# Typed gather pass of a graph network: weighting moved to the head of a turn, block indices and tables made one block ahead

## The chip, the cores and the metric

The kernel runs on one core of one Trainium2 chip. The metric is the device time of one execution in microseconds (us); lower is better. All names of engines are those of the profile: PE is the matrix engine, PEld its weight loads, DVE the vector engine, ACT the scalar engine, POOL the engine that issues the gathers, SP the one that issues plain transfers.

## The reference, cut to what matters

Four graph layers run one after the other on 12,500 nodes and 412,500 edges sorted by target node. The change lies in the first one, in its sum over edges:

```
W = einsum('rb,bio->rio', comp, basis)         # one 64x64 matrix for each of 64 edge types
msg = x[src] * edge_weight
s = segment_sum(msg, edge_type * N + dst)      # by type and target node
h = relu(einsum('rni,rio->no', s, W) + bias)
x = layernorm(x + batchnorm(h + relu(x @ res_w.T + res_b)))
```

The kernel first makes the table Yd of x times W for every node and type, so that the sum becomes, for each edge, the row Yd[src, type] times the edge's weight, added to the edge's target node. This sum over edges is the typed pass. The three later layers (two convolutions, then a pass over wide rows) use the same edges.

## The kernel before, in words

The program is a row of phases. `ytab` (to 560 us) builds Yd; `typed_pass` (lines 363 to 554, from 560 to 5688 us) makes the sum; then come `dense0` and the other layers, which the change doesn't touch.

The typed pass goes over 129 blocks of 25 times 128 edges (the last one has 23 times 128). Tiles are double buffered by j, the parity of the block. In every block there are two products of PE:

- **The groups.** For each of the 25 columns k of a block, PE multiplies two one-hot matrices (lines 527 and 529, a pair of matmuls) to build, in bf16, a matrix that later layers read back from DRAM. The one-hot matrices are written by DVE in 4 groups (`group`, lines 462 to 466: 6, 6, 6 and 7 columns) into a ring of two. PE waits for the group (semaphore gb). Every third column PE tells by a semaphore cm0, cm1 or cm2 that three columns are done ("a triple"; triples 0 to 8), ACT copies the triple out of PSUM (line 549), and PE may use that part of PSUM again two triples later (semaphore av). So column 24, the last of a block, waits for ACT's copy of triple 6. DVE may overwrite a part of the ring when the first triple of the following group is done: group 1 waits for triple 0, group 2 for triple 2, group 3 for triple 4, and group 0 of the next block for triple 6.
- **The sum by nodes.** POOL gathers 25 times 128 rows of Yd by the indices ix into gv (line 428), DVE multiplies them by the edge weights pw (line 501), DVE also writes the one-hot oh of the target nodes (line 491), and PE adds up gv times oh over the block (line 535, 50 records of f32 matmuls for 25 columns). The result is added to acc by DVE (`add`, line 471).

Each engine walks through the blocks in its own fixed order; `turn(b, j, i)` is one block on one engine, and `short_blocks` runs turn 0, a loop, and the last two turns.

DVE in turn b, before: group 0; `prep` for block b+1 (line 445 makes the indices ix, lines 447 to 455 the tables cl, vw, rl); group 1; the one-hot oh (line 491); group 2; `add` of block b-1; `weight` of block b+1 (line 474, into PSUM); group 3; the weighting of gv (line 501).

PE in turn b, before: the 25 pairs of the groups, then, when the weighting is done (semaphore mul), the sum by nodes, which ends with an increment of the semaphore pe.

POOL in turn b waits for pe of block b-2 (gv is free) and for ix of block b, and then issues 25 gathers.

SP in turn b, which isn't changed: it waits for pw of block b, issues the load of the table of block b+2 into mt[j] (line 398, 63.0 KB; source node, type, target, first target and weight of every edge), then waits for ACT's last copy of block b and issues the store of the block's matrix to Aj (line 405, 3062.5 KB). In the order of SP's stream the load for block b+2 thus stands right behind the store of block b-1:

```
def turn(b, j, i):
    if type(b) is not int or b + 2 < NA:
        b = reg(e, b)
        e.wait_ge(sm["pw"], reg(e, b + 1))
        load(b + 2, j)
    store(b, j, i)
```

Of the kernel before, what the change touches and what calls it, by code (L numbers as in the profile page):

```python
# [8 lines left out]
ALU = mybir.AluOpType  # L9
# [5 lines left out]
P = 128  # L15
# [15 lines left out]
KA = 25  # L31
NA = -(-E // (P * KA))
LA = -(-E // P) - (NA - 1) * KA
# [16 lines left out]
def build(nc, x, xT, meta, metaA, dstp, d0, d0s, jrow, half, dstr, wgt, efT, base, basa, ident, iota, basis, compT, l0v, res_wT,  # L50
          W1, l1b1, W2, l1b2, mW1, mb1, mW2, mb2, uW1, ub1, uW2, ub2, out):
    ctx = ExitStack()
    with ctx:
# [49 lines left out]
        def bc_f(v, t=NT, f=64):  # L103
            return v.unsqueeze(2).to_broadcast([P, t, f])

        def bc_t(v, t, f):
            return v.unsqueeze(1).to_broadcast([P, t, f])
# [40 lines left out]
        def at(b, n):  # L148
            return type(b) is int and b == n

        def reg(e, v):
            return v if type(v) is int else e.snap(v)
# [210 lines left out]
        def typed_pass(sm, block, s):  # L363
# [4 lines left out]
            gv = [big[:, KA * 65 * j:KA * 65 * (j + 1)].rearrange("p (k f) -> p k f", f=65) for j in range(2)]  # L368
            o0, o1 = KA * 130, KA * 130 + KA * P
            oh = big[:, o0:o1].rearrange("p (k n) -> p k n", n=P)  # L370
# [6 lines left out]
            rl = [loc(f"rl{j}", [P, KA]) for j in range(2)]  # L377
# [8 lines left out]
            ag = [PS[0][0:65, P * j:P * (j + 1)] for j in range(2)]  # L386
            pw = [PS[0][:, 2 * P + KA * j:2 * P + KA * (j + 1)] for j in range(2)]
            iof = PS[1][:, 0:W * NT]
# [44 lines left out]
            def vector(e):  # L433
                for h in range(4):
                    n = min(P, W * NT - P * h)
                    nc.vector.tensor_scalar(iof[:, P * h:P * h + n], io[:, 0:n], float(P * h), None,
                                            ALU.add).then_inc(sm["io"], 1)
                nc.vector.memset(oex[1][:, GM - 1, :], 0.0).then_inc(sm["io"], 1)
                nc.vector.memset(olo[1][:, GM - 1, :], 0.0).then_inc(sm["io"], 1)
                for j in range(2):  # L440
                    nc.vector.memset(gv[j][:, :, 64:65], 1.0).then_inc(sm["io"], 1)

                def prep(b, j, loaded, n):
                    e.wait_ge(sm[f"m{j}"], loaded)
                    nc.vector.scalar_tensor_tensor(out=ix[j][:, :], in0=mt[j][:, 0:KA], scalar=float(NR),
                                                   in1=mt[j][:, KA:2 * KA], op0=ALU.mult, op1=ALU.add).then_inc(sm["ix"], 1)
                    nc.vector.tensor_scalar(cl[j][:, 0:KA], mt[j][:, 0:KA], 7, None, ALU.logical_shift_right)
                    nc.vector.tensor_scalar(cl[j][:, KA:2 * KA], mt[j][:, 0:KA], P - 1, None, ALU.bitwise_and)
                    nc.vector.tensor_tensor(vw[j][:, 0:KA], mt[j][:, 2 * KA:3 * KA], mt[j][:, 3 * KA:4 * KA], ALU.subtract)
                    nc.vector.tensor_tensor(vw[j][:, KA:2 * KA], mt[j][:, 3 * KA + 1:4 * KA + 1], mt[j][:, 2 * KA:3 * KA],  # L450
                                            ALU.subtract)
                    nc.vector.tensor_tensor(rl[j][:, :], mt[j][:, 2 * KA:3 * KA], mt[j][:, 3 * KA:3 * KA + 1].to_broadcast([P, KA]),
                                            ALU.subtract).then_inc(sm["pr"], 1)
                    e.wait_ge(sm["pr"], n)
                    nc.vector.scalar_tensor_tensor(out=two(vw[j][:, :]), in0=two(vw[j][:, :]), scalar=float(NT),
                                                   in1=bc_t(cl[j][:, 0:KA], 2, KA), op0=ALU.mult,
                                                   op1=ALU.add).then_inc(sm["vw"], 1)

                def group(j, g, n):
                    r, k = g % 2, chunks[g]  # L460
                    m = k.stop - k.start
                    nc.vector.tensor_tensor(one[r][:, 0:m, :], bc_t(iof, m, W * NT), bc_f(vw[j][:, k], m, W * NT), ALU.is_equal)  # L462
                    nc.vector.tensor_tensor(oex[r][:, 0:m, :], bc_t(iof[:, 0:NT], m, NT),
                                            bc_f(vw[j][:, KA:2 * KA][:, k], m, NT), ALU.is_equal)
                    nc.vector.tensor_tensor(olo[r][:, 0:m, :], bc_t(iof[:, 0:P], m, P),  # L465
                                            bc_f(cl[j][:, KA:2 * KA][:, k], m, P), ALU.is_equal).then_inc(sm[f"gb{g}"], 1)

                def add(b, j):
                    at = e.value_load(basea[0:1, bass.ds(b, 1)], min_val=0, max_val=N)
                    dst = acc[0:65, bass.ds(at, P)]  # L470
                    nc.vector.tensor_tensor(dst, dst, ag[j], ALU.add).then_inc(sm["acc"], 1)

                def weight(j):
                    nc.vector.tensor_copy(pw[j], wgt_[j]).then_inc(sm["pw"], 1)

                def turn(b, j, i):
                    first, last, b = at(b, 0), at(b, NA - 1), reg(e, b)
                    n, c0, c1, c2 = reg(e, b + 1), reg(e, 3 * b), reg(e, 3 * b + 1), reg(e, 3 * b + 2)
                    kn = LA if last else KA
                    if not first:  # L480
                        e.wait_ge(sm["cm0"], c0)
                    e.wait_ge(sm["vw"], n)
                    group(j, 0, n)
                    if not first:
                        e.wait_ge(sm["mul"], b)
                    if not last:
                        prep(b + 1, 1 - j, 16 * (i + 1 + j), reg(e, b + 2))
                    e.wait_ge(sm["cm0"], c1)
                    group(j, 1, n)
                    e.wait_ge(sm["pe"], n)  # L490
                    nc.vector.tensor_tensor(oh[:, 0:kn, :], bc_t(iof[:, 0:P], kn, P), bc_f(rl[j][:, 0:kn], kn, P), ALU.is_equal)
                    e.wait_ge(sm["cm2"], c1)
                    group(j, 2, n)
                    if not first:
                        add(b - 1, 1 - j)
                    if not last:
                        weight(1 - j)
                    e.wait_ge(sm["cm1"], c2)
                    group(j, 3, n)
                    e.wait_ge(sm[f"g{j}"], 16 * KA * i + 16 * kn)  # L500
                    nc.vector.tensor_tensor(gv[j][:, 0:kn, 0:64], gv[j][:, 0:kn, 0:64], bc_f(pw[j][:, 0:kn], kn, 64),
                                            ALU.mult).then_inc(sm["mul"], 1)

                e.wait_ge(sm["io"], 8)
                prep(0, 0, 16, 1)
                weight(0)
                short_blocks(e, turn, NA)
                e.wait_ge(sm["pe"], NA + 1)
                add(NA - 1, 0)

            def tensor(e):
                e.sem_inc(sm["pe"], 1)

                def turn(b, j, i):
                    first, last, b = at(b, 0), at(b, NA - 1), reg(e, b)
                    n, done = reg(e, b + 1), [reg(e, 3 * b + h) for h in range(4)]
                    for k in range(LA if last else KA):
                        g, t = min(k // GC, GN - 1), k // 3
                        c = k - GC * g
                        r = g % 2  # L520
                        q = 2 + 3 * ((j + t) % 2) + k % 3
                        if c == 0:
                            e.wait_ge(sm[f"gb{g}"], n)
                        if k % 3 == 0:
                            if t >= 2 or not first:
                                e.wait_ge(sm[f"av{(t - 2) % 3}"], done[(t - 2) // 3 + 1])
                        nc.tensor.matmul(PS[q][:, 0:W * NT], olo[r][:, c, :], one[r][:, c, :], start=True, stop=False)  # L527
                        pr, pc = (r, c - 1) if c else (1 - r, GC - 1 if g else GM - 1)
                        mm = nc.tensor.matmul(PS[q][:, 0:NT], olo[pr][:, pc, :], oex[pr][:, pc, :], start=False, stop=True)  # L529
                        if k % 3 == 2 or k == (LA if last else KA) - 1:  # L530
                            mm.then_inc(sm[f"cm{t % 3}"], 1)
                    e.wait_ge(sm["mul"], n)
                    kn = LA if last else KA
                    for k in range(kn):
                        mm = nc.tensor.matmul(ag[j], gv[j][:, k, :], oh[:, k, :], start=(k == 0), stop=(k == kn - 1))  # L535
                    mm.then_inc(sm["pe"], 1)
                short_blocks(e, turn, NA)

            def scalar(e):
# [1161 lines left out]
```

## Time and profile before

| what | us |
| --- | --- |
| median of 3 runs | 13430.48 |
| lowest and highest run | 13422.02, 13433.54 |
| profiled execution, span from the first to the last instruction | 13426.1 |
| typed pass in it | about 560 to 5688 |
| busy in the span: PE, DVE, POOL, ACT | 7285.8, 6792.6, 6380.1, 2832.8 |

No separate time of the profiled execution beyond its span is shown; the span lies 4.4 us below the median of the runs. The page gives, for each engine, how long it was busy; in a timeline a row reads: start in us, duration in us, engine, line, operation, what it writes and reads, shapes, how many instructions were merged into the row, and in brackets how long the engine had been idle before and what released it. "Remote" as a releaser means a semaphore update that the profile can't tie to an instruction's end; "issue" means that it shows nothing that was waited for. Starts of matmuls are measured, their ends are modelled.

### The profile page before, as it was taken

Reading aid. Unit: us, or ns where it says so; the run is one execution under the profiler, and the core shown is the slowest. Engines: PE = TensorE matmul, PEld = TensorE weight load, DVE = VectorE, ACT = ScalarE, POOL = GpSimd, SP = SyncE. Lnnn points to the kernel's source line nnn. Section 1 sums busy time; section 2 is a strip of 40 time slices with the busy share of each in tenths; the row PEclk is TensorE's granted clock in tenths of the full one; section 3 lists DMA queues with packets and bytes.
Section 4 is the critical chain, followed back from the end, with each engine's and each line's share of the span. In section 5 each row is a group of like instructions: output and inputs, shape, how many; then the busy total and the mean of one; then the engine's idle time right before and its main releaser. Section 6 shows DMA issues by size and latency. Waiting matters only on the chain. (4 is left out here: it accounts for less than half of the span.)

```text
span 13426.1 us, 144231 instructions
## 1 busy us (share of the span) xinstructions
PE 7285.8 (54%) x52956; PEld 5571.9 (42%) x52956; DVE 6792.6 (51%) x8156; ACT 2832.8 (21%) x2654; POOL 6380.1 (48%) x6717
## 2 busy tenths in 40 slices
PE   9755545555555455589999994333333333333334
PEld 4333333333333333379989994222222222222223
DVE  5566666666666666632232224444444444444445
ACT  4333333333333333320000001111111111111112
POOL 4456565656565656400000004555555665555564
PEclk9877777677767666689999997666666666666667
DMA  9732323232323233379979994333333333333332
GB/s 388 290 107 97 106 97 106 98 106 98 106 97 106 97 105 99 106 267 370 370 292 370 371 370 116 87 88 88 88 86 85 87 88 88 87 88 87 85 86 66
DMA packets 480426, 2020.11 MB, mean 150 GB/s; under 512 B 193465, under 2 KB 246136, under 8 KB 354776
## 3 DMA queue, kind: packets, MB, share of 16 engines
q1 hardware_dynamic: 205304, 1283.59, 27.3%
q0 software_dynamic: 206272, 317.25, 10.1%
q10 hardware_dynamic: 68768, 418.23, 8.6%
q8 instruction: 46, 0.75, 0.0%
q14 instruction: 36, 0.29, 0.0%
HBM read 1385.92 MB, written 632.61 MB: 150 GB/s over the span
## 5 line engine op out<-in xcount | busy, mean ns | idle before, releaser
L1289 POOL DMA_INDIRECT big<-Pd,mt x3223 | 3041.0, 944 | 2127.8 <-DMA mt<-in_meta 1186.2
L428 POOL DMA_INDIRECT big<-Yd,ix x3223 | 3041.5, 944 | 2069.5 <-PE ps L535 1095.7
L462 DVE TENSOR_TENSOR ring<-ps,vw 128x2940 bf16<-128x2940 f32 (+1 forms) x516 | 1725.9, 3345 | 1761.8 <-PE ps L529 1516.3
L527 PE MATMUL ps<-ring 128*128 128x490 bf16 x3223 | 1427.4, 538 | 1999.5 <-DVE ring L465 1190.3
L1316 DVE TENSOR_TENSOR ps<-ps,big 128x1024 f32<-128x1024 f32 x403 | 494.9, 1229 | 2656.3 <-remote 2397.2
L527 PEld LDWEIGHTS ps<-ring 128*128 128x128 bf16 x3223 | 416.3, 129 | 2802.4 <-issue 1835.0
L1423 PE MATMUL ps<-idt,total 128*128 128x128 f32 x135 | 63.8, 473 | 2716.1 <-DVE total L1329 2716.1
L535 PE MATMUL ps<-big 128*65 128x128 f32 x6446 | 1149.9, 346 | 555.3 <-issue 554.6
L535 PEld LDWEIGHTS ps<-big 128*65 128x65 f32 x6446 | 1045.9, 185 | 651.7 <-issue 644.9
L1423 PEld LDWEIGHTS ps<-idt,total 128*128 128x128 f32 x135 | 24.4, 181 | 2814.7 <-DVE total L1329 2814.7
L549 ACT ACTIVATE Z<-ps 128x1470 bf16<-128x1470 f32 (+1 forms) x584 | 800.1, 1399 | 1790.2 <-PE ps L529 755.2
L549 ACT ACTIVATE big<-ps 128x1470 bf16<-128x1470 f32 (+1 forms) x576 | 786.5, 1397 | 1748.2 <-remote 833.6
L666 PE MATMUL ps<-big,cb 128*128 128x192 bf16 x12642 | 1065.5, 246 | 0.0
L666 PEld LDWEIGHTS ps<-big,cb 128*128 128x128 bf16 x12642 | 1036.4, 98 | 11.5
L1380 ACT ACTIVATE big<-ps 128x1024 bf16<-128x1024 f32 x269 | 275.2, 1023 | 2976.7 <-issue 2270.5
L529 PE MATMUL ps<-ring 128*128 128x98 bf16 x3223 | 850.5, 264 | 0.0
L1416 PE MATMUL ps<-big 128*128 128x384 bf16 x2151 | 565.9, 425 | 297.1 <-DVE big L1325 297.1
L1408 PE MATMUL ps<-qw,te 128*128 128x128 f32 x3216 | 510.3, 306 | 256.6 <-issue 256.4
L1115 POOL MEMSET acc<- 64x128 f32 x1 | 0.2, 198 | 1274.1 <-POOLq L115 1274.1
L1408 PEld LDWEIGHTS ps<-qw,te 128*128 128x128 f32 x3216 | 480.0, 222 | 260.1 <-issue 251.1
L1212 POOL TENSOR_TENSOR X<-X,vb 128x6272 f32<-128x6272 f32 x1 | 13.5, 13489 | 1174.2 <-POOLq L115 1174.2
L666 PE MATMUL ps<-big 128*128 128x192 bf16 x6370 | 550.0, 247 | 28.4 <-DMA big<-Aj 28.4
(215 smaller groups left out, 11561.0 us busy)
## 6 DMA issues: line engine op xcount, KB each, us to landing
Yd<-big SPq DMA_DIRECT2D x196, 1024.0 KB, 8.8
Aj<-Z SPq DMA_DIRECT2D x65, 3062.5 KB
big<-Aj SPq DMA_DIRECT2D x130, 1531.2 KB, 8.3
cb<-Aj ACTq DMA_DIRECT2D x130, 1531.2 KB, 8.5
Aj<-big SPq DMA_DIRECT2D x64, 3062.5 KB
cb<-Aj SPq DMA_DIRECT2D x128, 1531.2 KB, 8.4
Z<-Aj ACTq DMA_DIRECT2D x128, 1531.2 KB, 8.5
dr<-in_dstr SPq DMA_DIRECT2D x135, 1152.0 KB
```

Source lines behind the costliest of these rows:

```text
L428: e.indirect_dma_start(gv[j][:, k, 0:64], None, table, bass.IndirectOffsetOnAxis(ap=ix[j][:, k:k + 1], axis=0)).then_inc(sm[f"g{j}"], 16)
L462: nc.vector.tensor_tensor(one[r][:, 0:m, :], bc_t(iof, m, W * NT), bc_f(vw[j][:, k], m, W * NT), ALU.is_equal)
L527: nc.tensor.matmul(PS[q][:, 0:W * NT], olo[r][:, c, :], one[r][:, c, :], start=True, stop=False)
L529: mm = nc.tensor.matmul(PS[q][:, 0:NT], olo[pr][:, pc, :], oex[pr][:, pc, :], start=False, stop=True)
L535: mm = nc.tensor.matmul(ag[j], gv[j][:, k, :], oh[:, k, :], start=(k == 0), stop=(k == kn - 1))
L549: nc.scalar.activation(aw[j][:, :, 3 * t:3 * t + m, :], trip[(j + t) % 2][:, :, 0:m, :], ACT.Copy).then_inc(sm[f"av{t % 3}"], 1)
L666: last = nc.tensor.matmul(pa[j], buf[2 * j + h][:, D * c:D * c + P], wz[:, t, :], start=(t == 0), stop=(t == NT - 1))
L1289: e.indirect_dma_start(gv[j][:, k, :], None, Pd, bass.IndirectOffsetOnAxis(ap=mt[j][:, k:k + 1], axis=0)).then_inc(sm[f"g{j}"], 16)
L1316: nc.vector.tensor_tensor(step[q], step[q], G[j][:, SW * q:SW * (q + 1)], ALU.add).then_inc(sm[f"x{q}"], 1)
L1380: nc.scalar.activation(part[q][:, 0], step3[q], ACT.Relu).then_inc(sm[f"hi{q}"], 1)
L1408: last = nc.tensor.matmul(step[q][:, c * P:(c + 1) * P], te[j][:, k * P:(k + 1) * P], qw[j][k // HK][:, :], start=True, stop=True)
L1416: last = nc.tensor.matmul(ag, oh[j][:, k, :], parts[q][:, 3 * P * c:3 * P * (c + 1)], start=(k == 0), stop=(k == chunks - 1))
```

## The change

The reference and all phases but `typed_pass` stay as they are. Three engines' orders are touched:

- DVE, turn b, after: the weighting of gv of block b; `indices` of block b+2 (behind a wait for the load of that block's table); groups 0, 1, 2, 3 without anything between them; `prep` of the tables of block b+2; the one-hot oh of block b+1 (`targets`, behind a wait for PE's sum of block b); `add` of block b; `weight` of block b+2. Ahead of turn 0 the indices, tables and weights of blocks 0 and 1 and the one-hot of block 0 are made.
- PE, turn b, after: the sum by nodes of block b first, then the 25 pairs of block b.
- POOL, SP and ACT are as before.

```
-                def prep(b, j, loaded, n):
+                def indices(j, loaded):
                     e.wait_ge(sm[f"m{j}"], loaded)
                     nc.vector.scalar_tensor_tensor(out=ix[j][:, :], in0=mt[j][:, 0:KA], scalar=float(NR),
                                                    in1=mt[j][:, KA:2 * KA], op0=ALU.mult, op1=ALU.add).then_inc(sm["ix"], 1)
+
+                def prep(j, n):
                     nc.vector.tensor_scalar(cl[j][:, 0:KA], mt[j][:, 0:KA], 7, None, ALU.logical_shift_right)
...
+                def targets(j, n, kn):
+                    e.wait_ge(sm["pe"], n)
+                    nc.vector.tensor_tensor(oh[:, 0:kn, :], bc_t(iof[:, 0:P], kn, P), bc_f(rl[j][:, 0:kn], kn, P), ALU.is_equal)
+
                 def turn(b, j, i):
-                    first, last, b = at(b, 0), at(b, NA - 1), reg(e, b)
+                    first, last, more = at(b, 0), at(b, NA - 1), type(b) is not int or b + 2 < NA
+                    nxt = LA if at(b, NA - 2) else KA
+                    b = reg(e, b)
                     n, c0, c1, c2 = reg(e, b + 1), reg(e, 3 * b), reg(e, 3 * b + 1), reg(e, 3 * b + 2)
                     kn = LA if last else KA
+                    e.wait_ge(sm[f"g{j}"], 16 * KA * i + 16 * kn)
+                    nc.vector.tensor_tensor(gv[j][:, 0:kn, 0:64], gv[j][:, 0:kn, 0:64], bc_f(pw[j][:, 0:kn], kn, 64),
+                                            ALU.mult).then_inc(sm["mul"], 1)
+                    if more:
+                        indices(j, 16 * i + 32)
                     if not first:
                         e.wait_ge(sm["cm0"], c0)
                     e.wait_ge(sm["vw"], n)
                     group(j, 0, n)
-                    if not first:
-                        e.wait_ge(sm["mul"], b)
-                    if not last:
-                        prep(b + 1, 1 - j, 16 * (i + 1 + j), reg(e, b + 2))
                     e.wait_ge(sm["cm0"], c1)
                     group(j, 1, n)
-                    e.wait_ge(sm["pe"], n)
-                    nc.vector.tensor_tensor(oh[:, 0:kn, :], bc_t(iof[:, 0:P], kn, P), bc_f(rl[j][:, 0:kn], kn, P), ALU.is_equal)
                     e.wait_ge(sm["cm2"], c1)
                     group(j, 2, n)
-                    if not first:
-                        add(b - 1, 1 - j)
-                    if not last:
-                        weight(1 - j)
                     e.wait_ge(sm["cm1"], c2)
                     group(j, 3, n)
-                    e.wait_ge(sm[f"g{j}"], 16 * KA * i + 16 * kn)
-                    nc.vector.tensor_tensor(gv[j][:, 0:kn, 0:64], gv[j][:, 0:kn, 0:64], bc_f(pw[j][:, 0:kn], kn, 64),
-                                            ALU.mult).then_inc(sm["mul"], 1)
+                    if more:
+                        e.wait_ge(sm["gb3"], n)
+                        prep(j, reg(e, b + 3))
+                    if not last:
+                        targets(1 - j, reg(e, b + 2), nxt)
+                        add(b, j)
+                    if more:
+                        weight(j)
 
                 e.wait_ge(sm["io"], 8)
-                prep(0, 0, 16, 1)
-                weight(0)
+                for j in range(2):
+                    indices(j, 16)
+                    prep(j, j + 1)
+                    weight(j)
+                targets(0, 1, KA)
                 short_blocks(e, turn, NA)
...
                     n, done = reg(e, b + 1), [reg(e, 3 * b + h) for h in range(4)]
+                    e.wait_ge(sm["mul"], n)
+                    kn = LA if last else KA
+                    for k in range(kn):
+                        mm = nc.tensor.matmul(ag[j], gv[j][:, k, :], oh[:, k, :], start=(k == 0), stop=(k == kn - 1))
+                    mm.then_inc(sm["pe"], 1)
                     for k in range(LA if last else KA):
...
-                    e.wait_ge(sm["mul"], n)
-                    kn = LA if last else KA
-                    for k in range(kn):
-                        mm = nc.tensor.matmul(ag[j], gv[j][:, k, :], oh[:, k, :], start=(k == 0), stop=(k == kn - 1))
-                    mm.then_inc(sm["pe"], 1)
```

## Rows read from the trace of the kernel before

**Rows 1.** The page of the whole run: its span.

```profile
span 13426.1 us, 144231 instructions
```

**Rows 2.** Groups by line, 2000 to 5000 us: busy, mean ns | idle before, releasers.

```profile
L428 POOL DMA_INDIRECT big<-Yd,ix x1896 | 1789.0, 944 | 1211.7 <-PE ps L535 657.0 <-issue 554.7
...
L535 PE MATMUL ps<-big 128*65 128x128 f32 x3800 | 683.0, 348 | 326.9 <-issue 326.4
```

**Rows 3.** Timeline of one turn, all engines, 3009 to 3047 us.

```profile
3009.04 0.35 SPq L405 DMA_DIRECT2D Aj<-Z  x1
3009.93 0.34 SPq L398 DMA_DIRECT2D mt<-in_metaA  x1
...
3012.36 0.94 POOL L428 DMA_INDIRECT big<-Yd,ix  x1 [9.25 <-PE ps L535]
...
3012.76 3.22 DVE L462 TENSOR_TENSOR ring<-ps,vw 128x2940 bf16<-128x2940 f32 x1 [11.55 <-PE ps L529]
...
3017.44 3.48 DVE L491 TENSOR_TENSOR big<-ps,rl 128x3200 f32<-128x3200 f32 x1
...
3019.34 2.96 ACT L549 ACTIVATE big<-ps 128x1470 bf16<-128x1470 f32 x2 [3.74 <-issue]
...
3020.84 3.21 DVE L462 TENSOR_TENSOR ring<-ps,vw 128x2940 bf16<-128x2940 f32 x1
...
3025.51 0.28 DVE L471 TENSOR_TENSOR acc<-acc,ps 65x128 f32 x1
...
3027.34 3.73 DVE L462 TENSOR_TENSOR ring<-ps,vw 128x3430 bf16<-128x3430 f32 x1 [1.46 <-PE ps L529]
...
3032.76 1.81 DVE L501 TENSOR_TENSOR big<-big,ps 128x1600 f32<-128x1600 f32 x1
...
3034.26 0.29 PE L529 MATMUL ps<-ring 128*128 128x98 bf16 x1
...
3037.15 1.48 ACT L549 ACTIVATE big<-ps 128x1470 bf16<-128x1470 f32 x1 [6.86 <-remote]
3037.15 3.22 DVE L462 TENSOR_TENSOR ring<-ps,vw 128x2940 bf16<-128x2940 f32 x1 [2.58 <-remote]
...
3038.95 4.69 PE L535 MATMUL ps<-big 128*65 128x128 f32 x26
...
3042.32 0.95 POOL L428 DMA_INDIRECT big<-Yd,ix  x1 [0.30 <-issue]
...
3042.49 0.21 DVE L455 SCALAR_TENSOR_TENSOR vw<-vw,cl 128x50 f32<-128x50 f32 x1
...
3046.94 4.05 PE L535 MATMUL ps<-big 128*65 128x128 f32 x22 [0.38 <-issue]
3046.96 2.10 ACT L549 ACTIVATE big<-ps 128x1470 bf16<-128x1470 f32 x2 [8.33 <-remote]
```

**Rows 4.** Transfers, 3010 to 3016 us: packets, bytes, packets by size.

```profile
DMA packets 98, 2.40 MB, mean 400 GB/s; under 512 B 0, under 2 KB 0, under 8 KB 0
```

**Rows 5.** Transfers, 3017 to 3019 us: packets by size, then SP's queue.

```profile
DMA packets 289, 0.20 MB, mean 99 GB/s; under 512 B 224, under 2 KB 224, under 8 KB 289
...
q1 hardware_dynamic: 160, 0.06, 11.6%
```

**Rows 6.** Timeline of the first turns, 563 to 602 us.

```profile
563.17 3.19 SPq L398 DMA_DIRECT2D mt<-in_metaA  x3
...
565.03 0.19 DVE L445 SCALAR_TENSOR_TENSOR ix<-mt 128x25 int32<-128x25 int32 x1 [0.62 <-DMA mt<-in_metaA]
...
602.00 1.48 ACT L549 ACTIVATE Z<-ps 128x1470 bf16<-128x1470 f32 x1 [13.22 <-remote]
```

**Rows 7.** Timeline of the pass's end, 5675 to 5690 us.

```profile
5675.55 6.50 PE L535 MATMUL ps<-big 128*65 128x128 f32 x46
5677.68 0.34 SPq L405 DMA_DIRECT2D Aj<-Z  x1
...
5689.24 0.51 SPq L892 DMA_DIRECT2D wA<-in_res_wT  x1
```

## The prediction, made before the changed kernel had run

> **What bounds the kernel now.** The span is 13426.1 us [rows 1]; I make the sum against it, and add the 4.4 us by which the median of the runs (13430.5) lies above it. A measurement of this kernel can tell about 0.2% (27 us) from no change. Only the typed pass is touched.
>
> First the groups by line [rows 2]. In 3000 us POOL waited for PE's sum by nodes (line 535) in 76 turns (1896 gathers at 25 a turn), so a turn takes 3000 / 76 = 39.5 us, and these waits come to 657.0 / 76 = 8.6 us a turn. A chain that holds both POOL and PE thus sets the turn. The timeline of a turn shows it [rows 3]:
>
> - Gathers start at 3012.36, released by the end of the sum, and the last is issued at 3042.32: 30.9 us of gathering.
> - PE's record for the last matmul of triple 6 starts at 3034.26 and should be done near 3034.5, yet ACT and DVE, both waiting for it, start at 3037.15. ACT's copy of triple 7 starts only at 3046.96, though all matmuls but column 24 stood ready behind it. In the same time the sum by nodes issues 26 matmuls from 3038.95, falters, and runs the last 22 in one piece from 3046.94. So PE's completions are held back while gathers go on, from about 22 us after their start, and come free at 3046.96, 34.6 us after it. I have no name for the mechanism, but it follows the gathers: in the first turns, where gathering began near 566 and didn't pause, ACT's copy came 13.22 us late at 602.00 [rows 6]; in the last turn, without any gathers, the sum runs through, 46 matmuls in 6.50 us [rows 7].
>
> The turn before is then 34.6 (gathers and hold) + 4.05 (the 22 last matmuls) + 0.85 (to the next gather) = 39.5 us, as observed. DVE has slack: its idle 11.55 us ahead of 3012.76.
>
> **The change part by part.** PE's stream is the same ring of sum, groups, sum, groups; only its cut into turns moves. POOL's two gates are met in the same place: indices exist long before, and the sum releases it. The instructions of DVE are the same in number, so nothing is saved or added in busy time. What moves:
>
> 1. *The one-hot oh (3.4 us) leaves the gap between groups 1 and 2.* Call x the start of group 1 (3012.76). Group 1 ends at x+4.8 (3017.53). Group 2 then waits for triple 2 (ACT starts on it at 3019.34): x+6.6, instead of 3020.84. Group 2 takes 4.7 (3020.84 to 3025.51, where `add` begins), then 1.8 for triple 4 (to 3027.34), then group 3 takes 5.5: it ends at x+18.6 instead of x+20.1. Gain 1.5 us. `add` and `weight` (0.28 and about as much less, 0.5 together at most) were covered by the 1.8 and are now open.
> 2. *The tail of DVE's turn.* Tables 0.8 (group 0, indices and tables run from 3037.15 to 3042.70, less 4.7 for the group), oh 3.4, add and weight 0.5, weighting 1.81 [rows 3]: the weighting ends at x+25.1, and the sum may start then. Before, the weighting ended at x+21.8 and the sum started at x+26.2, behind column 24. This gives the gain of 1. back.
> 3. *The indices.* One instruction of 0.18 us, but with a wait in front that DVE didn't have to pay: the table of block b+2. SP issues that load 0.9 us behind the store of block b-1 (3009.04, 3009.93), which itself waits for ACT's last copy of block b-1. Between 3010 and 3016 the queues carry 98 packets, all of the store's large size [rows 4]; the load's small ones (160 on SP's queue, 0.06 MB) come between 3017 and 3019 [rows 5]. I take the landing at 3018.3, 8.4 us after issue; the bounds are 1.9 us, for a load with no store before it (563.17 to 565.03) [rows 6], and 11.6 us, the last store to the next phase's first issue [rows 7]. I stay with 8.4 because the load stands in exactly this place in every turn. With 1.9 the turn is that of rivals (c) and (d), with 11.6 group 1 moves 3 us further into the gathers, which is rival (b). Before, this landing had almost a whole turn of cover. Now DVE stands at the wait from x+25.1, and behind it in DVE's order are group 0 and every later group, for which PE and ACT wait in turn.
>
> The new chain without any hold: ACT's last copy (triple 6 at x+20.3, then 1.48, 1.48 and 0.72) ends at x+24.0; store and load are issued by x+25.0; landing x+33.4; indices and group 0 (0.2 and 4.7, as group 2) x+38.3; triple 0 on PE 1.7: next x at x+40.0. The sum by nodes lies beside this wait (x+25.2 to about x+33) and costs nothing any more. So 40.0 us a turn is the floor, against 39.5.
>
> With the hold: group 1 now starts later after the gathers' start, so more of the groups falls into the held stretch. The last triples come free 34.6 us after the gathers' start. From there: ACT's copy of triple 6 1.5, column 24 0.5, the whole sum 8.0, next gathers 0.85. I take 8.0 between 50/46 of 6.50 = 7.1 [rows 7] and 50 x 683.0/3800 = 9.0 [rows 2]. A turn: 34.6 + 2.0 + 8.0 + 0.85 = 45.4 us; I use 45.2, since triple 7 sometimes comes 1 us sooner. It closes on itself: next x lies 3.7 (ACT) + 9.4 (store, load, landing) + 4.9 + 1.7 = 19.7 behind the release, the gathers start 10.8 behind it, so x is 8.9 us into the gathers (before: 0.4), triple 6 would be due at 29.2, well after 22, and is held to 34.6. What was worth 4.05 us behind the release, since half of the sum was already issued, is now the whole sum and column 24.
>
> Turns 1 to 126 pay this: 126 x (45.2 - 39.5) = +718 us. The ends: the groups of block 0 no longer run beside the first gathers, but the first sum ends some 4 us sooner; at the end, the groups of block 128 follow its sum and the last store (10.6 us to land) follows them: about +37. In all 718 + 33 = +751: span 14177, median 14181; I say 14180.
>
> The Trainium skill, DMA: Bandwidth & Descriptors, section Anatomy of one DMA, gives 2.0 us plus bytes over 436 KB a us, an estimate of 2.1 us for the load; group 1 would then start some 2.6 us into the gathers and the turn would stay near 39.5: no change. The same page, section Queues, rings and completion order, has the descriptors of one issuing engine consumed in ring order, and with that rule the packets of rows 4 and 5 agree.
>
> **The rivals.** (a) *The load wait without the hold.* If completions aren't held where the groups now fall, a turn takes 40.0: +63 + 33, median 13527. Against it: all late triples in rows 3 and 6. Chance 0.14. (b) *The hold reaches triple 4.* It is due 8.9 + 13.1 = 22.0 us into the gathers, just where the hold began; then group 3 starts at the release and a turn takes about 52.5. If this hits half of the turns, 48.9 in the mean: +1184 + 33, median 14650. Chance 0.14. (c) *The load is there in time* (it would have to land by x+25.2; decides: a landing of 2 us after issue or less). With the hold as before, a turn stays at 39.5 and only the ends count, +33 or less, 13430 to 13463; chance 0.06. The rule of the Trainium skill, DMA: Bandwidth & Descriptors, section Anatomy of one DMA, would bring this case about. (d) *Faster.* The load in time, and with the weighting and the sum away from triples 6 to 8 the sum isn't held: weighting x+25.1, sum to x+33.2, triple 0 to x+35. A turn of 35.0 gives -567 + 33, median 12896; it decides if the store no longer stands before the load and the release moves ahead of the sum. For it speaks only that PE is idle half of the time. Chance 0.07. (e) The change doesn't do what it says: the indices are early in the program but not in time, since their load isn't; this is the forecast.
>
> **How the numbers follow.** Forecast 0.59; (a) 0.14, (b) 0.14, (c) 0.06, (d) 0.07. The forecast's own range, with 7.1 and 9.0 for the sum and 33.8 to 34.6 for the release, is 44.1 to 46.5 a turn, 14040 to 14350. The range reaches to (a) and (b): 13500 to 14700. Slower by over 0.2%: 0.59 + 0.14 + 0.14, with a third of (c), 0.89; within 0.2%: 0.04; faster: 0.07.
>
> **What would show it.** Right: in the changed profile POOL's gathers start every 45 us; DVE has an idle stretch of 6 to 10 us before the indices, ended by the load of mt; the sum runs in one piece of some 8 us; ACT's copies of triples 6 and 7 start together with the release, about 34.5 us after the gathers' start. Wrong: no idle time before the indices (landing), triples 6 and 7 on time although gathers go on (hold), or turns of 39.5 us or less.

## The result, and the profile after

The changed kernel takes 14581.2 us (4 runs, 14578.7 to 14583.7) against 13432.0 for the kernel before (4 runs, 13422.0 to 13436.1): a ratio of 1.0855, interval 1.084 to 1.087. It is slower, as forecast, and within the range (13500 to 14700), but by 1149 us where 750 were forecast. The profiled execution has a span of 14579.0 us.

The page, in the lines that answer to [rows 1] and to the groups that matter:

```profile
span 14579.0 us, 144292 instructions
...
L428 POOL DMA_INDIRECT big<-Yd,ix x3223 | 3041.0, 944 | 3195.1 <-DVE ix L445 2243.1
...
L445 DVE SCALAR_TENSOR_TENSOR ix<-mt 128x25 int32<-128x25 int32 x129 | 24.1, 186 | 2102.5 <-DMA mt<-in_metaA 2102.5
```

The gathers had waited for PE's sum [rows 2]; now they wait for the indices, and DVE stands 2102.5 / 129 = 16.3 us a turn in front of the indices' instruction, for the load of mt. The same groups from 2000 to 5000 us:

```profile
L428 POOL DMA_INDIRECT big<-Yd,ix x1547 | 1459.5, 943 | 1542.4 <-DVE ix L445 1089.9 <-issue 452.6
...
L531 PE MATMUL ps<-big 128*65 128x128 f32 x3100 | 464.2, 322 | 0.0
```

1547 gathers at 25 a turn are 61.9 turns, 3000 / 61.9 = 48.5 us each. Of them POOL waits 1089.9 / 61.9 = 17.6 for the indices. A turn took 39.51 before (taken here and below as the mean distance of two stores over the whole loop; after: 48.47), and 126 x (48.47 - 39.51) = +1129 of the 1149. The rest, 20, is the ends. The busy time of DVE is nearly what it was (6827.3 against 6792.6), so the change didn't add work: it added a wait.

The timeline of the changed kernel shows the turn, which answers to [rows 3]; its columns are the same. "Hold" stands below for what the prediction describes: while gathers go on, what PE has finished by its records reaches ACT and DVE late. "The release" is the moment at which it comes free.

```profile
3002.54 0.34 SPq L398 DMA_DIRECT2D mt<-in_metaA  x1
...
3010.69 0.19 DVE L445 SCALAR_TENSOR_TENSOR ix<-mt 128x25 int32<-128x25 int32 x1 [16.35 <-DMA mt<-in_metaA]
3010.90 3.22 DVE L464 TENSOR_TENSOR ring<-ps,vw 128x2940 bf16<-128x2940 f32 x1
3011.66 0.94 POOL L428 DMA_INDIRECT big<-Yd,ix  x1 [17.62 <-DVE ix L445]
...
3017.48 3.22 DVE L464 TENSOR_TENSOR ring<-ps,vw 128x2940 bf16<-128x2940 f32 x1 [1.82 <-PE ps L545]
...
3031.03 3.73 DVE L464 TENSOR_TENSOR ring<-ps,vw 128x3430 bf16<-128x3430 f32 x1 [2.20 <-PE ps L545]
...
3031.62 0.29 PE L545 MATMUL ps<-ring 128*128 128x98 bf16 x1
...
3037.29 3.48 DVE L480 TENSOR_TENSOR big<-ps,rl 128x3200 f32<-128x3200 f32 x1
3040.69 0.28 DVE L473 TENSOR_TENSOR acc<-acc,ps 65x128 f32 x1
3040.85 1.49 ACT L560 ACTIVATE big<-ps 128x1470 bf16<-128x1470 f32 x1 [8.34 <-remote]
3040.98 1.81 DVE L489 TENSOR_TENSOR big<-big,ps 128x1600 f32<-128x1600 f32 x1
...
3046.51 3.45 ACT L560 ACTIVATE big<-ps 128x1470 bf16<-128x1470 f32 x3 [4.17 <-remote]
3048.52 7.81 PE L531 MATMUL ps<-big 128*65 128x128 f32 x50
3050.13 0.35 SPq L405 DMA_DIRECT2D Aj<-big  x1
3050.67 0.34 SPq L398 DMA_DIRECT2D mt<-in_metaA  x1
3059.17 0.19 DVE L445 SCALAR_TENSOR_TENSOR ix<-mt 128x25 int32<-128x25 int32 x1 [16.39 <-DMA mt<-in_metaA]
3060.14 0.94 POOL L428 DMA_INDIRECT big<-Yd,ix  x1 [17.57 <-DVE ix L445]
```

Read it from one start of the gathers to the next:

- 3011.66 to 3046.51, **34.85 us**: gathers and hold. ACT's copies of triples 6 to 8 run in one piece from 3046.51, released by no matmul's end ("remote").
- to 3050.13, **3.62**: the three copies, at whose end SP issues the store.
- to 3050.67, **0.54**: SP issues the load behind it (0.89 in the turn before this one, 3001.65 to 3002.54).
- to 3059.17, **8.50**: the load lands; the indices.
- to 3060.14, **0.97**: the first gather.

The sum is 48.48 us. PE's sum by nodes runs from 3048.52 to 3056.33 in one piece and is over 2.84 us before the indices. So it gates nothing.

Triple 5 is held too, which the prediction didn't have: its last matmul (3031.62) should be done 20.3 us into the gathers, and ACT copies it at 3040.85. The turn doesn't depend on it, since triple 6 waits for the release in any case.

The granted clock of PE in 2000 to 5000 us is 0.61, against 0.70 before. No matmul ends one of the stretches in the list above, and load_early_b (below) has 0.62 at a turn of 39.5, so the clock isn't what makes the turn longer.

The transfers of the changed kernel from 3003 to 3009 us, and from 3010 to 3011 us, are as in [rows 4, 5]: the store's large packets go first, and the load's small ones come when it is through.

```profile
DMA packets 100, 2.45 MB, mean 408 GB/s; under 512 B 0, under 2 KB 0, under 8 KB 0
```

```profile
DMA packets 154, 0.06 MB, mean 64 GB/s; under 512 B 154, under 2 KB 154, under 8 KB 154
```

### The profile page after: what moved, and what is told of

It reads as the page before. It is cut to its first block and busy times, and to the rows that moved or that the text cites. A ratio compares the mean times of both kernels' runs of the same rounds, so it can differ in the third digit from the quotient of the medians.

```text
span 14579.0 us, 144292 instructions
## 1 busy us (share of the span) xinstructions
PE 7362.5 (51%) x52956; PEld 5514.2 (38%) x52956; DVE 6827.3 (47%) x8156; ACT 2833.5 (19%) x2654; POOL 6379.0 (44%) x6717
## 5 line engine op out<-in xcount | busy, mean ns | idle before, releaser
L543 PE MATMUL ps<-ring 128*128 128x490 bf16 x3223 | 1636.1, 599 | 3566.8 <-DVE ring L467 1907.8
L543 PEld LDWEIGHTS ps<-ring 128*128 128x128 bf16 x3223 | 445.8, 138 | 4557.6 <-issue 2947.5
L445 DVE SCALAR_TENSOR_TENSOR ix<-mt 128x25 int32<-128x25 int32 x129 | 24.1, 186 | 2102.5 <-DMA mt<-in_metaA 2102.5
L531 PE MATMUL ps<-big 128*65 128x128 f32 x6446 | 972.0, 323 | 72.5 <-DVE big L489 48.9
L531 PEld LDWEIGHTS ps<-big 128*65 128x65 f32 x6446 | 944.6, 171 | 111.4 <-issue 61.9
L545 PE MATMUL ps<-ring 128*128 128x98 bf16 x3223 | 921.5, 286 | 1.8 <-issue 1.5
```

## The experiments

Three readings stood after this. **The load**: the 9 us a turn are the wait for the load, which the hold passes on. **The order**: it is the new order of DVE's work (oh, tables and add ahead of the weighting, the sum behind it), and the load's wait is only where it shows. **PE itself**: the hold doesn't follow the gathers, and the late copies come from PE's own stream.

One thing has to be known for the numbers. In the first four runs (load_early, before_g12, after_g12, load_early_g12) the unchanged kernel before, run beside them, took 11280.0 us (7 runs, 11278.2 to 11281.7); in the eight others it took 13436.9 (7 runs) and 13435.7 (12 runs), as in the first measurement. The profiles fit this: in load_early no copy of ACT is late, in load_early_b, the same program, they are. The first four were thus made **without the hold**, the others with it. Each run is compared only with runs of its own condition.

**load_early**: the load is issued a store earlier (block b+3 instead of b+2, ahead of the store of block b), so that it has a whole turn to land.

```
-    if type(b) is not int or b + 2 < NA:
+    if type(b) is not int or b + 3 < NA:
         b = reg(e, b)
-        e.wait_ge(sm["pw"], reg(e, b + 1))
-        load(b + 2, j)
+        e.wait_ge(sm["pw"], reg(e, b + 2))
+        load(b + 3, 1 - j)
     store(b, j, i)
 ...
 load(1, 1)
+e.wait_ge(sm["pw"], 1)
+load(2, 0)
```

> Edit to the changed kernel: SP issues the table of block b+3 ahead of the store of block b, so the load that DVE waits for has been under way for a whole turn. Theory (load wait plus hold): the 16 us wait before the indices is gone, the gathers are released by the end of PE's sum again, and the turn is set by gathers, hold and the rest of the sum as in the kernel before: 38 to 41 us a turn, 13250 to 13650 us. Rival 1 (the new order of PE's stream costs, the load only looks guilty): the turn stays near 48.5 us, 14500 us or more. Rival 2 (with the sum at the head the hold no longer bites): 35 us a turn, 12850 to 12950 us.

Measured: 11681.7 us, 1.0355 of the kernel before (interval 1.0338 to 1.0373), turn 34.1 us. The expectation was for the condition with the hold, and this isn't it; against 11280 it shows that without the hold the change costs some 3 us a turn even if the load is early. Its groups by line, 2000 to 4000 us:

```profile
L430 POOL DMA_INDIRECT big<-Yd,ix x1465 | 1383.4, 944 | 617.9 <-issue 428.3 <-PE ps L533 189.6
...
L533 PE MATMUL ps<-big 128*65 128x128 f32 x2944 | 495.6, 349 | 137.3 <-DVE big L491 137.3
```

POOL waits for the sum again, but the sum waits for DVE's weighting (137.3 us in 59 turns, 2.3 each). I put this down to the new order of DVE's work, at a size of 3 us and not 9; no run without the hold changes the order alone.

**before_g12, after_g12, load_early_g12**: the same three kernels with 12 gathers a block instead of 25. The 13 others aren't made; the weighting takes the preset ones in their place, and all else is unchanged.

```
-for k in range(LA if at(b, NA - 1) else KA):
+for k in range(12):
     e.indirect_dma_start(
 ...
-e.wait_ge(sm[f"g{j}"], 16 * KA * i + 16 * kn)
+e.wait_ge(sm[f"g{j}"], 16 * 12 * i + 16 * 12)
```

> The kernel before with 12 gathers a block instead of 25; part of the sum over edges is left out. Theory: its turn of 39.5 us is gathers plus hold plus the rest of the sum; without the hold it is 20.5 us to the end of group 3, 4 for triple 6 to column 24, 8 for the sum and 0.85, 33 to 34 us a turn: 12600 to 12750 us. Rival (the gap in the sum isn't caused by the gathers): no change, 13400 us.

> The changed kernel with 12 gathers a block instead of 25; the sum takes 13 columns that were never gathered, so part of the sum over edges is left out. Theory: gathering lasts 15 us, so no completion of the late triples is held, and what remains is the load chain without hold, 40.0 us a turn: 13450 to 13600 us. Rival (the late triples are held by something else than the gathers, say PE's own order or its clock): still 46 to 49 us a turn, 14250 us or more.

> The changed kernel with the early load and 12 gathers a block; part of the sum over edges is left out. Theory: neither load wait nor hold; weighting at 25.1, sum 8, first triple 1.7, a turn of 34.5 to 35.5 us: 12800 to 12950 us, so in itself the new order is 1 to 2 us a turn slower than the old one. Rival (the new order is the better one once nothing else is in the way): at or below the kernel before with 12 gathers.

Measured: 11215.8, 12393.9 and 11665.8 us; turns of 30.7, 39.9 and 34.1 us. Two steps are told apart: from 39.9 to 34.1, 5.7 us, is the load's wait, and 34.1 - 30.7 = 3.4 us is what else the change did, the new order. after_g12 comes out at the prediction's own floor without a hold, 40.0. load_early_g12 and load_early differ by 16 us (0.1%): without the hold, half of the gathers less is worth nothing there. The hold was missing for the 25 gathers too, so these runs alone don't say that 12 gathers avoid it; that is what before_g12_b and after_g12_b are for. load_early_g12 wasn't made with the hold.

**before_again, after_again**: the two kernels unchanged.

> The kernel before, unchanged, for a profile beside the other kernels of this call. The last call's kernel before took 11280 us, not 13430, and its relatives showed no late completions at all, although 25 gathers went on. Theory now: the hold belongs to a condition of the first measurement, not to the gathers alone. If the condition is absent again: 31 to 31.5 us a turn, limited by 25 gathers at 1.25 us, and no copy of ACT later than 0.2 us after its matmuls. If it is present: 39.5 us a turn, 13430 us.

> The changed kernel, unchanged. Theory: without the hold the load chain sets the turn, as it did with 12 gathers: 39.8 us a turn, 12370 to 12430 us, 1.095 to 1.10 of the kernel before. Rival (the chain of gathers behind the indices counts on top): 43 us or more a turn, 12850 us or more. With the hold present: 48.5 us a turn, 14580 us.

Measured: 13445.2, turn 39.6; and 14584.8, ratio 1.0852 (1.0834 to 1.087), turn 48.5. The hold is there again, and the result repeats.

**load_act**: the changed kernel, but the load is issued by ACT, at the beginning of its turn b. This changes two things: the queue, and the order in time. ACT issues the load while its last copies of block b-1 run, 0.4 to 2.1 us ahead of the store in every turn; in the changed kernel SP issues it 0.5 to 0.9 us behind the store.

```
 # SP
-    if type(b) is not int or b + 2 < NA:
-        b = reg(e, b)
-        e.wait_ge(sm["pw"], reg(e, b + 1))
-        load(b + 2, j)
     store(b, j, i)
 # ACT
+    if type(b) is not int or b + 2 < NA:
+        b = reg(e, b)
+        e.wait_ge(sm["pw"], reg(e, b + 1))
+        e.dma_start(mt[j][:, :], metaA[b + 2]).then_inc(sm[f"m{j}"], 16)
```

> Edit to the changed kernel: the load of the table of block b+2 is issued by ACT, right behind its last copy of block b-1, and so on another queue than the store and not behind it. Theory: the landing of 8.4 us was the queue behind 3062.5 KB of store. With no store ahead it is about 2 us: DVE's wait shrinks from about 8 us to 2, the turn from 39.8 to 34.1 us, about 11690 us. Rival (the 16 transfer engines are busy with the store whichever queue issues): the landing stays at 5 us or more and the turn at 37 to 40 us, 12050 us or more.

Measured: 13648.1 us (one run; 1.016 of before), turn 41.0. The expectation was again written for the other condition; with the hold, its point is the landing. The timeline of load_act:

```profile
3028.41 0.34 ACTq L554 DMA_DIRECT2D mt<-in_metaA  x1
...
3029.73 0.33 SPq L405 DMA_DIRECT2D Aj<-big  x1
3030.31 0.19 DVE L441 SCALAR_TENSOR_TENSOR ix<-mt 128x25 int32<-128x25 int32 x1 [9.33 <-DMA mt<-in_metaA]
...
3036.86 0.94 POOL L424 DMA_INDIRECT big<-Yd,ix  x1 [13.42 <-PE ps L527]
```

From issue to indices it is 1.9 us, not 8.4, and POOL is released by PE's sum again (line 527 there). 7.4 of the 9 us a turn are gone, though the load isn't issued a turn earlier. So the price is the store ahead of the load. Whether another queue is needed for it, or only the place ahead of the store, this run doesn't tell: the load's packets are through before the store moves its first (in other turns the two overlap by at most 0.3 us). Transfers of load_act by queue, 3028 to 3030.5 us:

```profile
q10 hardware_dynamic: 144, 0.06, 11.3%
```

The store's packets (q1) start at 3030.56. The rival, that the store keeps the transfer engines busy for every queue, therefore stands, and the kernel before speaks for it. There the gathers, on a queue of their own (q0), start at 3012.36 while a store is moving. The transfers of before, first 3012.3 to 3017.8 us, then 3017.8 to 3018.6:

```profile
q1 hardware_dynamic: 148, 1.99, 92.8%
...
big<-Yd,ix POOLq DMA_INDIRECT x5
```

```profile
q0 software_dynamic: 125, 0.13, 59.7%
```

Five gathers are issued and not one of their packets moves until the store is through, 5.5 us after the first gather's start (the median of 120 turns). In the changed kernel, where no store is moving then, it is 1.65 us in every turn looked at. A load behind the store on ACT's queue might wait as well; no run has one.

**oh_mid**: load_early, with the one-hot and `add` moved back between groups 1 and 2.

```
 group(j, 1, n)
+if not last:
+    targets(1 - j, reg(e, b + 2), nxt)
+    add(b, j)
 e.wait_ge(sm["cm2"], c1)
```

> Edit to the changed kernel with the early load: the one-hot of block b+1 and the add of block b stand between groups 1 and 2, where the one-hot stood in the kernel before. Theory: the wait for triple 2 (1.8 us) covers half of it, and the tail of DVE's turn, for which PE's sum waits, is 3.7 us shorter: 34.1 to 32 to 32.5 us a turn, 11450 to 11500 us. Rival (the tail isn't the limit): 34 us or more, since 1.5 us are added between the groups.

Measured: 13419.3 us (one run), turn 39.2. It was made to undo the cost of the order, which shows only without the hold; with the hold it lies 0.13% below the kernel before, which one run can't tell from no change. So nothing follows for the order, and there is no version here that beats the kernel before for certain.

**load_early_b, before_g12_b, after_g12_b**: three of the first kernels once more, now with the hold.

> The changed kernel with the load of the table a block earlier, again. Hold present, theory: gathers released by PE's sum, the turn set by gathers, hold and the rest of the sum as in the kernel before, 39 to 41 us, 13400 to 13650 us; the load wait is then all of the 9 us a turn. Rival (half of the 9 us is the order of the stream): 43 us or more a turn, 13900 us or more. Without the condition: 34.1 us a turn, 11680 us.

> The kernel before with 12 gathers a block again (part of the sum over edges is left out), since the first time no kernel of that call had late completions. Two conditions have been seen, by whole calls: with the hold (kernel before 13430 us) and without (11280 us). If it is present: theory (the hold needs some 22 us of gathering): the typed pass runs at 30.7 us a turn as it did without the hold, while the wide pass with its 24 gathers keeps its 37.6, 12250 to 12300 us. Rival (the condition holds PE's completions whatever POOL does): 37 us or more a turn, 13100 us or more. Without the condition: 11216 us again.

> The changed kernel with 12 gathers a block again (part of the sum over edges is left out). Hold present, theory: 39.8 us a turn, the load chain alone, 13400 to 13480 us; of the 48.5 us of a turn of the changed kernel the hold is then 8.7. Rival (the hold bites at 12 gathers too): 43 us or more a turn. Without the condition: 12394 us again.

Measured: load_early_b 13451.0 us, ratio 1.0012 (1.0003 to 1.0022), turn 39.5; before_g12_b 12289.8, turn 30.7; after_g12_b 13463.4, turn 39.9. The groups of load_early_b, 2000 to 4000 us:

```profile
L430 POOL DMA_INDIRECT big<-Yd,ix x1266 | 1194.5, 944 | 806.2 <-PE ps L533 435.9 <-issue 370.3
...
L447 DVE SCALAR_TENSOR_TENSOR ix<-mt 128x25 int32<-128x25 int32 x51 | 8.9, 175 | 0.0
```

The indices have no idle time ahead of them any more, POOL waits for the sum (435.9 / 50.6 = 8.6 us a turn, to the tenth what it was before [rows 2]), and the turn is that of before. With the hold, then, the whole 9.0 us a turn of the change are the wait for the load, and the 3.4 us of the order don't show. Why they don't isn't taken apart: the release isn't at one fixed time there, for triple 7 is copied 24 to 35 us after the gathers' start (30.2 in the mean, 34.4 in the kernel before).

before_g12_b is the same program as before_g12, and its turn is the same within 0.01 us, though the runs beside it with 25 gathers show the hold. Its timeline:

```profile
3007.44 0.94 POOL L428 DMA_INDIRECT big<-Yd,ix  x1 [16.04 <-PE ps L535]
...
3029.20 3.22 DVE L462 TENSOR_TENSOR ring<-ps,vw 128x2940 bf16<-128x2940 f32 x1
...
3031.20 6.09 PE L535 MATMUL ps<-big 128*65 128x128 f32 x50
3038.16 0.94 POOL L428 DMA_INDIRECT big<-Yd,ix  x1 [16.04 <-PE ps L535]
```

Group 0 of the next block, which triple 6 releases, starts 21.8 us after the gathers did, and the sum runs in one piece. After 12 gathers (14.7 us of them) nothing is held; with 25 (30.9 us) it is, from about 20 us (the triple 5 of the changed kernel). In after_g12_b, too, that triple is copied on time, at 20.3 us. That speaks against PE itself as the cause: its stream is the same with 12 and with 25. And the condition is still there, in a later phase of these same two programs; the groups by line of the whole run, first before_g12, then before_g12_b:

```profile
L1316 DVE TENSOR_TENSOR ps<-ps,big 128x1024 f32<-128x1024 f32 x403 | 481.7, 1226 | 1598.8 <-DMA big<-Pd,mt 1598.8
```

```profile
L1316 DVE TENSOR_TENSOR ps<-ps,big 128x1024 f32<-128x1024 f32 x403 | 495.1, 1229 | 2658.5 <-remote 2389.6 <-issue 257.3 <-DMA big<-Pd,mt 10.9
```

The idle time ahead of this one instruction grows from 1598.8 to 2658.5 us, and its releaser turns from a DMA into "remote". That and its busy time (+13) are 1073 of the 1074 us between 11215.8 and 12289.8; the typed pass has no part in it. So the condition isn't a matter of PE's completions alone: here it is DVE that waits for gathered data.

after_g12_b is the load's chain alone. Its timeline is the prediction's rival (a) step by step: group 1 starts at 2999.49, which is x; the last copy ends at x+23.9 (24.0 said), the load is issued at x+25.0 (25.0) and has landed at x+33.2 (33.4).

```profile
2999.49 3.22 DVE L464 TENSOR_TENSOR ring<-ps,vw 128x2940 bf16<-128x2940 f32 x1 [1.82 <-PE ps L545]
...
3019.84 3.58 ACT L560 ACTIVATE Z<-ps 128x1470 bf16<-128x1470 f32 x3 [4.41 <-PE ps L545]
3023.59 0.35 SPq L405 DMA_DIRECT2D Aj<-Z  x1
3024.47 0.34 SPq L398 DMA_DIRECT2D mt<-in_metaA  x1
...
3032.64 0.19 DVE L445 SCALAR_TENSOR_TENSOR ix<-mt 128x25 int32<-128x25 int32 x1 [8.32 <-DMA mt<-in_metaA]
3033.61 0.94 POOL L428 DMA_INDIRECT big<-Yd,ix  x1 [25.22 <-DVE ix L445]
...
3039.43 2.95 ACT L560 ACTIVATE big<-ps 128x1470 bf16<-128x1470 f32 x2 [16.02 <-PE ps L545]
```

**idx_after_g0**: the changed kernel, with the wait for the load and the indices behind group 0 instead of ahead of it.

```
-if more:
-    indices(j, 16 * i + 32)
 if not first:
     e.wait_ge(sm["cm0"], c0)
 e.wait_ge(sm["vw"], n)
 group(j, 0, n)
+if more:
+    indices(j, 16 * i + 32)
```

> Edit to the changed kernel: the wait for the load and the indices stand behind group 0 instead of ahead of it; the load stays where it is. Theory: group 0 is built while the load is under way, group 1 starts right behind the indices, and triple 6 falls before the hold. Hold present: 35 from the gathers' start to the release of triple 7, two copies 2.2, store and load 0.7, landing 8.4: 46 to 47 us a turn, 14260 to 14400 us. Without it: 34 to 35 us a turn, 11680 to 11800 us. Rival (the gathers' start behind the landing is all that counts): 48.5 and 39.8 as in the changed kernel.

Measured: 14134.3 us (one run), turn 44.9, 1 to 2 us less than expected. Its groups, 2000 to 4000 us:

```profile
L428 POOL DMA_INDIRECT big<-Yd,ix x1111 | 1048.3, 944 | 947.1 <-DVE ix L445 622.0 <-issue 325.2
...
L445 DVE SCALAR_TENSOR_TENSOR ix<-mt 128x25 int32<-128x25 int32 x44 | 8.2, 187 | 681.3 <-DMA mt<-in_metaA 681.3
```

POOL is still gated by the indices, 622.0 / 44.4 = 14.0 us a turn. Group 0 no longer stands behind the landing, so all groups come some 7 us earlier in the gathers (triple 4 is copied 12.2 us after their start in the mean, 19.1 in the changed kernel), and only the last triples meet the hold: triple 7 is copied at 30.3 and triple 8 at 34.0, where in the changed kernel the copies of triples 6 to 8 begin at 34.8. I had expected the full hold for them too; that was the miss. From triple 8 on the turn adds up as before: 34.0 + 0.7 (its copy) + 1.1 (store, load) + 8.2 (landing) + 1.0 = 45.0.

## Why the prediction was right, and where it was short

**The direction and the mechanism** held. DVE waits for the load of mt, the load sits behind the store, groups move into the held stretch, and the release is 34.8 us after the gathers' start where 34.6 was said. The landing is 8.35 us in the mean (8.4 said), the weighting ends 25.3 us behind the start of group 1 (25.1 said), the sum starts 2.0 us behind the release (2.0 said) and takes 7.8 in one piece (8.0 said), the ends are +20 us (+33 said). The shift in the order of DVE's tail, step 1 and 2, was said to come out even; without the hold it costs 3.4 us, with it nothing that shows.

**The step that failed** is the sentence "POOL's two gates are met in the same place: indices exist long before, and the sum releases it". They don't. The gathers of turn b+2 need the indices that now lie behind the load's landing, and the prediction had all that is needed to see it: it put the landing 3.7 + 9.4 = 13.1 us behind the release, and the next gathers 10.8 us behind it, that is, before their own indices. With 34.6 + 13.1 + 0.2 + 0.85 the same terms give 48.8 us a turn; 48.5 was measured. The step was written for the kernel before, where the indices have a turn of cover, and wasn't looked at again when that cover was gone. It is worth 48.47 - 45.2 = 3.27 us a turn, 126 times, 412 us: all of the 401 us by which the time was missed, with 13 given back at the ends and the rest rounding. That the time still fell into the stated range is due to rival (b), which had stretched the range upwards; the forecast's own range ended at 14350.

Two signs followed from it. Group 1 begins 5.8 us into the gathers (3017.48 less 3011.66) and not 8.9, since the gathers themselves start later. DVE's idle stretch before the indices is 16.4 us and not 6 to 10: that figure was taken from the chain without a hold (33.4 less 25.1), while with it the copies after the release belong to it. By the prediction's own terms it should have read 47.7 less 34.0 = 13.7, from the weighting's end to the landing.

Two smaller things were off and moved nothing. The hold was said to begin about 22 us into the gathers; it reaches triple 5 at 20.3. And the lower end of the forecast's own range, 44.1 a turn, is by its terms 33.8 + 2.0 + 7.1 + 0.85 = 43.8.

**The rivals.** (a), the load's wait without the hold, 40.0 us a turn, is what after_g12 and after_g12_b show (39.9 in both), where the gathering is too short for a hold; of the whole kernel it isn't true. (b), 48.9 us a turn, has nearly the number that came out, and not the mechanism: triple 4 is copied 19.1 us after the gathers' start, on time, and group 3 starts at 3031.03, 15 us before the release. Its number and that of the missing gate only happen to meet. (c) and (d) fell, for the load lands in 8.4 us. The rule that the prediction put behind (c), 2.0 us plus bytes over 436 KB a us in the Trainium skill's DMA: Bandwidth & Descriptors, section Anatomy of one DMA, is given there for DMAs that GpSimd issues, and this load comes from SP or ACT. Its 2.1 us (an estimate) still fit the load with nothing ahead of it, 1.9 us in load_act; behind the store it takes 8.4. By the same page's section Queues, rings and completion order, each transfer engine consumes the descriptors of one issuing engine in ring order, and the packets of the changed kernel agree. They would look the same if the store held up every queue, as the gathers of the kernel before suggest (load_act above).

**The sum of causes**, from the turns. With the hold: 48.5 less 39.5 (load_early_b) = 9.0 us for the load's wait; or, seen from the other side, 48.5 less 39.9 (after_g12_b) = 8.6 us for the hold, since in the changed kernel the two are in series. The two don't add up to a whole; each is what goes when that cause alone is taken away. Without the hold: 5.7 us for the wait (after_g12 less load_early_g12) and 3.4 for the order.

**What stays open.** Why the hold is there at one time and not at another, with the same program on the same chip, no run tells; nor what it is. Shown is only that it needs both the condition and more than 14.7 us of gathering without a pause, and that it delays what other engines wait for while PE's records look on time. The changed kernel itself wasn't run without the hold. Nor is it told apart whether the load waits for the store because both are in SP's queue, or would wait on any.

## What to carry to other kernels

A wait that moves to an earlier place in an engine's order has to be priced for every engine that reads what stands behind it: list each consumer, and ask of each whether its gate is still the old one, with the landing put in. A small load behind a large store costs the store's time; before moving a consumer up, have the load issued ahead of the store (7.4 us a turn here, from ACT) or a turn earlier (9.0 us). When two gates lie within some microseconds of each other, work out both ends and take the later one.

## What the runs showed of the hardware that was not expected

- The same program took 11280 us beside the first four experiments and 13436 beside the others, with a spread of at most 0.3% each time. With 12 gathers a block in the typed pass the difference is 1074 us, nearly all of it in a later phase where DVE waits for gathered data, released by "remote" instead of a DMA. The rest, 2156 less 1074, some 1080 us, would be the typed pass with its 25; this is an estimate, since no profile of the kernel before without the hold was kept.
- With the hold, what PE has finished by its records reaches ACT and DVE late once gathers have run for about 20 us: triple 5 of the changed kernel by 8.9 us in the turn shown, by up to 12 in others (13 in [rows 6]). All is free some 35 us after their start (34.8 for triple 6 of the changed kernel), some 4 us after the last of the 25 has ended. With 12 gathers it doesn't happen (before_g12_b: 21.8 us for triple 6, on time).
- A 63 KB load lands in 1.9 us when it is issued 0.4 to 2.1 us ahead of a 3 MB store (load_act), and in 8.35 us in the mean behind it (8.1 to 10.4).
- The gathers' packets, on another queue than the store, begin 1.65 us after the first gather's start when no store moves (changed kernel), and 5.5 us after it, at the store's end, when one does (before).
